# Attention and feed-forward kernel, Trainium2: the row of maxima by a DMA instead of a matmul and a VectorE copy, and the correction passes reordered around it

## What is computed

```python
Q = jnp.einsum('bnd,hdk->bhnk', x, proj_q)
K = jnp.einsum('bmd,dk->bmk', x, proj_k)
V = jnp.einsum('bmd,dv->bmv', x, proj_v)
logits = jnp.einsum('bhnk,bmk->bhnm', Q, K)
weights = jax.nn.softmax(logits, axis=-1)
O = jnp.einsum('bhnm,bmv->bhnv', weights, V)
Y = jnp.einsum('bhnv,hdv->bnd', O, proj_o)
# feed-forward, without a nonlinearity, 8 experts summed
mid = jnp.einsum('amh,ehn->aemn', x, w1)
out = jnp.einsum('aemn,enh->amh', mid, w2)
```

## Time and profile before

| | us |
|---|---|
| median of 3 runs | 1636.69 (1636.4 to 1636.76) |
| the profiled execution | 1637.05 |
| its span in the trace | 1635.2 |
| PE busy | 1618.8 (99%) |
| POOL busy | 1379.3 (84%) |
| ScalarE (ACT) busy | 1300.6 (80%) |
| VectorE (DVE) busy | 1229.2 (75%) |

### The profile page before, as it was taken

One profiled execution on the slowest core, in us unless ns is written; L12 is line 12 of the kernel. 1 busy time (PEld: TensorE's weight loads), 2 busy tenths in 40 slices (PEclk: granted clock), 3 DMA queues, 4 the chain that ended last, 5 costly groups with the idle time before them and its releaser, 6 DMA issues.

```text
span 1635.2 us, 46288 instructions
## 1 busy us (share of the span) xinstructions
PE 1618.8 (99%) x18686; PEld 1199.7 (73%) x18686; DVE 1229.2 (75%) x2605; ACT 1300.6 (80%) x1348; POOL 1379.3 (84%) x1008
## 2 busy tenths in 40 slices
PE   8999999999999999999999999999999999999998
PEld 6777777777777777777777777777777777777775
DVE  6777777777777777777777777777777777777775
ACT  4788888888888888888888888888888888878885
POOL 3688888888888888888888888888888888888786
PEclk9999999999999999999999999999999999999999
DMA  8000000000000000000000000000000000000000
GB/s 237 4 3 5 5 4 18 4 4 5 4 17 5 4 5 5 16 5 5 4 5 18 3 5 5 4 18 4 4 5 3 18 5 3 4 14 2 2 2 14
DMA packets 34690, 20.41 MB, mean 12 GB/s; under 512 B 18353, under 2 KB 30897, under 8 KB 34481
## 3 DMA queue, kind: packets, MB, share of 16 engines
q1 hardware_dynamic: 33440, 16.92, 3.9%
q10 hardware_dynamic: 1040, 0.52, 0.1%
HBM read 9.57 MB, written 4.19 MB: 8 GB/s over the span
## 4 chain that ended last, share of the span: by engine, by line
PE 97%; DVE 1%; ACT 1%; issue 0%; ACTq 0%; POOL 0%; DVEq 0%
PE s_ps L599 14%; PE s_ps L614 14%; PE s_ps L612 14%; PE t_ps L654 13%; PE t_ps L657 13%; PE t_ps L656 13%; PE s_ps L483 4%; PE s_ps L485 4%; PE s_ps L484 4%; PE t_ps L636 2%; PE t_ps L627 1%; PE t_ps L669 0%; PE s_ps L627 0%; DVE c_lo L970 0%; ACT pr_hi L446 0%; DVE xn L772 0%
## 5 line engine op out<-in xcount | busy, mean ns | idle before, releaser
L348 POOL TENSOR_TENSOR pr_lo<-pr,pr_hi 128x1024 f16<-128x1024 f32 x511 | 1079.6, 2135 | 228.3 <-ACT pr_hi L446 228.3
L439 ACT ACTIVATE pr<-s_ps,boost,scale 128x1024 f32<-128x1024 f32 x512 | 616.4, 1204 | 193.7 <-PE s_ps L614 193.6
L865 DVE TENSOR_REDUCE key_max<-s_ps 128x128 f16<-128x1024 f32 x512 | 624.0, 1219 | 0.2 <-PE s_ps L599 0.2
L446 ACT ACTIVATE pr_hi<-pr 128x1024 f16<-128x1024 f32 x512 | 525.5, 1051 | 8.2
L612 PE MATMUL s_ps<-g_lo,xT 128*128 128x128 f16 x4096 | 512.4, 219 | 1.0 <-DVE g_lo L878 1.0
L614 PE MATMUL s_ps<-g_hi,xT 128*128 128x128 f16 x4096 | 512.4, 219 | 0.0
L612 PEld LDWEIGHTS s_ps<-g_lo,xT 128*128 128x128 f16 x4096 | 400.4, 98 | 31.5 <-DVE g_lo L878 1.5
L614 PEld LDWEIGHTS s_ps<-g_hi,xT 128*128 128x128 f16 x4096 | 400.5, 98 | 29.9
L654 PE MATMUL t_ps<-pr_hi,xn_hi 128*128 128x512 f16 x1024 | 388.2, 379 | 1.8 <-DVE pr_lo L883 1.8
L657 PE MATMUL t_ps<-pr_hi,xn_lo 128*128 128x512 f16 x1024 | 388.2, 379 | 0.0
L656 PE MATMUL t_ps<-pr_lo,xn_hi 128*128 128x512 f16 x1024 | 388.2, 379 | 0.0
(11 more groups left out here) (126 smaller groups left out, 1545.3 us busy)
## 6 DMA issues: line engine op xcount, KB each, us to landing
out_dram<-xacc SPq DMA_DIRECT2D x16, 256.0 KB, 2.7
w_sb<-in_L_ffn_w_dram SPq DMA_DIRECT2D x1, 2048.0 KB, 9.5
xT<-xn_hi SPq DMA_TRANSPOSE x56, 2.2
xT<-xn_lo SPq DMA_TRANSPOSE x56, 2.4
pr<-in_L_attn_proj_q_dram ACTq DMA_DIRECT2D x1, 512.0 KB, 4.6
xacc<-in_L_attn_x_dram SPq DMA_DIRECT2D x2, 256.0 KB, 5.0
pr<-in_L_attn_proj_o_dram SPq DMA_DIRECT2D x1, 512.0 KB, 6.5
xacc<-in_L_attn_x_dram SPq DMA_DIRECT2D x1, 384.0 KB, 10.4
```

The lines of the kernel that those rows point to most:

```text
L348: pool.tensor_tensor(pr_lo[:, u % RING, :], pr32[:, u % PR, :], pr_hi[:, u % RING, :], ALU.subtract)\
L439: act.activation(pr32[:, u % PR, :], both_banks(u), ACT.Exp, bias=boost[:, 0:1], scale=scale[:, 0:1])\
L446: act.activation(pr_hi[:, u % RING, :], pr32[:, u % PR, :], ACT.Copy).then_inc(p_hi_ready, 1)
L865: dve.tensor_reduce(key_max[:, u % 2, :], both_banks(u).rearrange("p (t q) -> p q t", q=P), AX_X, ALU.max).then_inc(keys_max, 1)
```

## The change

The column of maxima is no longer turned by TensorE and copied by VectorE; SP waits for it and writes it as a row of 128 float16 numbers into row 0 of g_lo by a DMA from the 128 partitions. `low_passes` is cut into `low_keys` (keys' low by g_hi, needs no maximum) and `low_queries` (keys' high by g_lo, waits for the DMA). `low_keys` stands where the low passes began (in P1 it stands behind the projection, as before), `low_queries` stands late in the period, in P0, P1 and P3 behind the first product of place 1, in P2 behind all three. In P2 the first chunk of a block gives two products ahead of `turn_keys_max` instead of one. On VectorE `find_max` comes ahead of `between_maxima` in P1 and P2. SP runs one loop over the units: the bias DMA of each, a transpose at positions 1 and 2 of eight, the stores at positions 5 and 6 of every eighth pair.

```diff
-        minus_max = sb("minus_max", [P, 2, P], F16)
+        minus_max = sb("minus_max", [P, 2], F16)
...
+            def bias(u):
+                k, j = divmod(u, 4)
+                sp.wait_ge(max_found, u + 1)
+                if j == 0:
+                    sp.wait_ge(g_lo_ready, k + 1)
+                if u >= 1:
+                    sp.wait_ge(bias_in, 16 * u)
+                sp.dma_start(g_lo[0:1, k % 2, j * P:(j + 1) * P], minus_max[:, u % 2:u % 2 + 1]).then_inc(bias_in, 16)
...
+            for u in range(UNITS):
+                bias(u)
+                pair, at = divmod(u, 8)
+                if pair == 1 and at in (4, 5, 6, 7):
+                    turn(NT + at // 2 - 2, at % 2)
+                if at in (1, 2) and pair >= 2 and (tile := ln_tile(pair - 2)) is not None:
+                    turn(tile, at - 1)
+                batch = pair // H - 1
+                if pair % H == 2 and at in (5, 6) and batch >= 0:
+                    store(batch, at - 5)
...
-            def low_passes(u):
+            def low_keys(u):
                 k, j = divmod(u, 4)
-                pe.wait_ge(bias_ready, u + 1)
+                pe.wait_ge(keys_max, u + 1)
+                for t in range(NT):
+                    pe.matmul(bank(u, t // HT)[:, (t % HT) * P:(t % HT + 1) * P], x_lo(batch_tile(k) + t),
+                              g_hi[:, k % 2, j * P:(j + 1) * P], start=False, stop=False, skip_group_check=True)
+            def low_queries(u):
+                k, j = divmod(u, 4)
+                pe.wait_ge(bias_in, 16 * (u + 1))
                 if j == 0:
                     pe.wait_ge(g_lo_ready, k + 1)
                 for t in range(NT):
...
                 last.then_inc(scores_ready, 1)
...
             def turn_keys_max(u):
                 pe.wait_ge(keys_max, u + 1)
                 if u >= 1:
-                    pe.wait_ge(bias_ready, u)
+                    pe.wait_ge(max_found, u)
...
+                if u % 4 == 3 and summing(u - 1) >= 0:
+                    pe.wait_ge(t_lo_ready, summing(u - 1) + 1)
...
-            def max_to_row(u):
-                pe.wait_ge(max_found, u + 1)
...
                 if n < UNITS:
                     high_pass(n, 0)
-                if 1 <= n <= UNITS and at != 3:
-                    max_to_row(n - 1)
-                if n < UNITS:
                     high_pass(n, 1)
-                if 1 <= n <= UNITS and at == 3:
-                    max_to_row(n - 1)
                 if n == 0:
                     fold_c(1)
                 chunk(n, 0)
-                small_products(n)
+                if at == 1:
+                    small_products(n)
                 if 1 <= n <= UNITS:
-                    low_passes(n - 1)
+                    low_keys(n - 1)
+                if at != 1:
+                    small_products(n)
                 if at == 2:
-                    chunk(n, 1, rest=False)
+                    chunk(n, 1, (0, 1))
                 if n < UNITS:
                     turn_keys_max(n)
-                chunk(n, 1, first=at != 2)
+                chunk(n, 1, (2,) if at == 2 else (0,))
+                if 1 <= n <= UNITS:
+                    low_queries(n - 1)
+                if at != 2:
+                    chunk(n, 1, (1, 2))
...
             def find_max(u):
                 dve.wait_ge(turned, u + 1)
-                dve.tensor_reduce(minus_max[:, u % 2, 0:1], maxima_turned(u), AX_X, ALU.max, negate=True)\
+                if u >= 2:
+                    dve.wait_ge(bias_in, 16 * (u - 1))
+                dve.tensor_reduce(minus_max[:, u % 2:u % 2 + 1], maxima_turned(u), AX_X, ALU.max, negate=True)\
                    .then_inc(max_found, 1)
-            def place_bias(u):
...
             for n in range(PERIODS):
-                if 1 <= n <= UNITS:
-                    place_bias(n - 1)
                 if n < UNITS:
                     max_of_keys(n)
-                between_maxima(n)
+                if n % 4 in (0, 3):
+                    between_maxima(n)
                 if n < UNITS:
                     find_max(n)
+                if n % 4 in (1, 2):
+                    between_maxima(n)
```

More of the change, by code:

```diff
@@ L131, in attention_ffn @@
         g_ps, g_hi_ready, g_lo_ready = sem("g_ps"), sem("g_hi_ready"), sem("g_lo_ready")
-        high_done, keys_max, turned, max_found, rowed, bias_ready = (
-            sem(n) for n in ("high_done", "keys_max", "turned", "max_found", "rowed", "bias_ready"))
+        high_done, keys_max, turned, max_found, bias_in = (
+            sem(n) for n in ("high_done", "keys_max", "turned", "max_found", "bias_in"))
         scores_ready, exp_done, p_hi_ready, p_lo_ready = (
@@ L610, in low_passes @@
                 for t in range(NT):
[L611 to L615, removed]
+                    last = pe.matmul(bank(u, t // HT)[:, (t % HT) * P:(t % HT + 1) * P], x_hi(batch_tile(k) + t),
+                                     g_lo[:, k % 2, j * P:(j + 1) * P], start=False, stop=True, skip_group_check=True)
                 last.then_inc(scores_ready, 1)
@@ L626, in turn_keys_max, with weigh @@
                     pe.wait_ge(w1_evacuated, E)
+                if u % 4 == 3 and summing(u - 1) >= 0:
+                    pe.wait_ge(t_lo_ready, summing(u - 1) + 1)
                 pe.transpose(maxima_turned(u), key_max[:, u % 2, :], ident16[:, :]).then_inc(turned, 1)
-            def max_to_row(u):
-                pe.wait_ge(max_found, u + 1)
[L631 to L639, removed]
+            def weigh(k, t, products):
                 tile = (batch_tile(k) + t) % KEEP
@@ L644, in weigh @@
                 dst = sum_bank(k).rearrange("p (j c) -> p j c", j=4)
-                if first:
+                if 0 in products:
                     if t == 0:
@@ L650, in weigh @@
                             pe.wait_ge(t_lo_ready, k - 1)
-                        pe.wait_ge(bias_ready, min(4 * k + 6, UNITS))
+                        pe.wait_ge(max_found, min(4 * k + 6, UNITS))
                         if k == 1:
@@ L672, in fold_ffn, with chunk @@
                     last.then_inc(f_ps, 1)
-            def chunk(n, place, first=True, rest=True):
-                if n < 4 and rest:
+            def chunk(n, place, products=(0, 1, 2)):
+                if n < 4 and 2 in products:
                     turn_w1(2 * n + place)
-                if n in FOLDS and rest:
+                if n in FOLDS and 2 in products:
                     for e in range(2):
@@ L684, in chunk @@
                 if 0 <= k < BLOCKS:
-                    weigh(k, t, first, rest)
+                    weigh(k, t, products)
             def head_out(k, g):
```

26 lines of the change are left out of this document (9 added, 17 removed).

## The result

| | before | after |
|---|---|---|
| median, us | 1636.59 (4 runs) | 1773.34 (4 runs, 1771.54 to 1775.42) |
| ratio | | 1.0835, 95% interval 1.0822 to 1.0848 |
| span of the profiled execution, us | 1635.2 | 1771.3 |

Forecast were 1720 us, range 1700 to 1765: the direction was right, the size was not.

A forecast was written before the change was run, and what follows sets the result against it. PE, 99% busy, was taken as the bound, but after the change the loop behind W sets the pace: 54 blocks of 13.54 and 72 of 12.71 us give +82.1, with the end +83.2, so 1720 us; range 1700 to 1765.

The forecast's parts named there:

- the loop behind W: From W, a block's first weighing product in P2, through exponentials, p_high and POOL to the next: 13.54 or 12.71 us.
- the 1.15: In P2, late low_queries start the exponentials 1.35 instead of 0.20 us behind the first weighing product, lengthening the loop by 1.15.
- the hop back to PE: From the end of POOL's last p_low to PE's next first weighing product: between 0 and 0.14 us, taken as 0.05.
- The DMA: Bias copy from find_max's end to PE's start: bounded at 2.0 to 2.9 us, taken as 2.3, stalling PE 0.1 a block.
- The rooms: Time from find_max's end until low_queries is due, by unit: 2.3, 2.2, 2.5 and over 3.4 us.
- the rival that was worked out for 2.9: Bias DMA slow too, about 2.9 us: PE's blocks 13.2 and 13.35, short blocks +0.5, total 1755 us; chance 0.15.
- The start: Up to the first weighing product: 0.3 us of row matmuls saved, set against the first DMA landings; no net change.
- SP: SP's queue of bias DMAs, transposes and stores: a bias delayed by 0.5 us vanishes in PE's wait; nothing.
- The row matmuls and VectorE's copies: 512 row matmuls off PE save 28.7 us only if PE stays the bound; VectorE's copies, 142.8 us busy, no gain themselves.
- max_of_keys and the early turn: In P3 and P0 turn_keys_max comes at 1.89 us, its maximum ready at 1.90; 0.1 a block allowed.
- The end: From the last but one block's first weighing product to the last's: about 11.7 instead of 10.57 us, +1.1.
- What the profile would show: PE idle before the first weighing product, some 115 us, POOL's pr_lo as releaser; chain full of POOL's p_low.

The follow-up runs named there:

- the order alone: Kernel before, row matmul and VectorE copy kept, no bias DMA; only TensorE's order changed to that of the change: 1731.44 us, ratio 1.0576.
- the kernel with four pieces: Changed kernel with VectorE's 32 by 32 block transpose behind find_max, so the bias DMA moves four 64-byte runs: 1741.38 us, ratio 1.0637.
- the probes: Changed kernel with extra small DMAs of various shapes on the sync queue, to time their landings; kernel time not of interest, landings 1.55 to 2.8 us.
- the best kernel: Changed kernel with four 64-byte pieces, ScalarE's p_high ahead of the exponentials in P2, and the 3 MB x load in six parts: 1631.35 us, ratio 0.9967.

## Why the prediction was wrong in size, step by step

- **What bounds the kernel, and the loop behind W: right.** The chain was read correctly. The run with the order alone reproduces its length with the 1.15 added: 13.59 and 12.77 measured, 13.54 and 12.71 forecast. The term that was off is the hop back to PE, 0.10 where 0.05 was taken; over 126 blocks that is 6.3 us. The sum also took the first block as one of its kind; it is 3.0 longer (15.73 with the order alone; 14.54 before).
- **The DMA: the step that failed.** "I bound it at 2.0 to 2.9 ... and take 2.3, next to the transposes, whose payload is smallest." It took 2.86 from find_max's end to low_queries. The rooms were right (2.3, 2.2, 2.5, over 3.4; in the kernel with four pieces, where it hardly waits for the DMA, TensorE comes 2.38, 2.37, 2.45 and 3.41 behind find_max's end), and so was the rival that was worked out for 2.9, with its chance of 0.15: "PE's blocks become 13.2", measured 13.18, and "It decides from about 2.7 on". What failed was the choice inside the bounds by size in bytes. By the probes bytes don't decide at this size (one run of 256 B lands in 1.7, 512 B in pieces of four bytes in 1.9), while the shape does: a column of two-byte pieces written into a row takes 1.1 more than a column into a column. In 71 blocks without a normalisation this is 13.18 less 12.77, some 29 us; over all blocks, against the order alone, it is 1688.0 - 1656.2 = 31.8.
- **The fixed cost that the Trainium skill gives** for a DMA on GpSimd's path (DMA: Bandwidth & Descriptors, "Anatomy of one DMA — SWDGE (gpsimd) path", about 2.0 us) is near three of the four shapes here, 1.7 to 2.0 on SP's queue, and 0.8 below the one that the kernel uses. For that one the measurement decides.
- **The start: failed.** "The first landings have turn_w1 and the folds as cover, and I set the two against each other." The cover was there for a landing of 3 us. The queue was not looked at: the first bias DMA stood behind 3 MB of loads and landed after 12.2, and the clock fell to its lower level within the wait. The start got 11.1 us longer, where the prediction set it at nothing; the run with the load in six parts returns 10.3 of them. The range's upper end, 1765, had room for the slow DMA (1755 by its rival); without these 11.1 us the time would have been 1762.
- **SP: right otherwise.** A transpose or a store behind a bias does not lengthen its landing (median 2.78 with and 2.77 without). What did, by up to 0.7 in one unit of ten, goes with the instruction queues' packets, which the prediction doesn't mention.
- **The row matmuls and VectorE's copies: right as "no gain by itself".** The 28.7 us off PE were there and bought nothing as long as two longer loops stood.
- **max_of_keys and the early turn, "next to nothing; I allow 0.1 a block":** right for the changed kernel, where VectorE's copies are gone (11.4 us in front of the turn, 0.09 a block). In the kernels that kept them it was more: the run that puts the turn later in P3 returns 27.4 us, 0.21 a block.
- **The end: right**, 11.72 against about 11.7.
- **What the profile would show: partly wrong.** The chain does not run through POOL, since the waits of this kind are given as "issue", and PE waits mostly before low_queries: 120 us there by the distances between its starts, 19 in front of W, in 49 blocks, where some 115 were forecast. The waits for the DMA fall in the same blocks and use up most of what POOL's loop leaves. By the prediction's own test this meant that the DMA decides, which is true for the blocks without a normalisation.

The forecast's +83.2, plus 9.9 for the loop as the order alone shows it (1656.2 instead of 1646.3: the hop, the first block and some hundredths), 31.8 for the DMA and 11.1 for the start, give 136.0 of the 136.1. So two steps failed, the DMA's duration and the start set at nothing; the loop, the larger part, was right.

## What to carry to other kernels

A bound at 97 to 99% busy can have a second loop a tenth of a microsecond behind it: before an operation is moved, follow what it releases all the way round to the next wait of the bound engine, through every engine's written order, and write down the slack. For a small DMA in such a loop look at the shape, not the bytes: here 128 two-byte pieces into one partition were the slow one, and four runs gathered by VectorE the fastest. What the gathering engine does next comes later for it, so follow that as well. And look at what stands on its queue when it is issued for the first time.

## What the runs showed of the hardware that was not expected

- A copy of 128 two-byte pieces landed in 1.7 us from column to column, in 2.0 from row to column and in 2.8 from column to row, all 256 bytes on SP's queue. One run of 256 bytes took 1.7.
- From a column into one partition, 32 and 64 two-byte pieces took 1.90 and 2.14, but 128 four-byte pieces only 1.89 and four 64-byte pieces 1.55.
- All 51 of the later biases that landed after more than 2.95 us (3.5 at most) had packets of the instruction queues running beside them; of the 298 without such packets none took that long.
- A DMA issued behind a 3 MB load on the same queue landed after 12.2 us, though it moved 256 bytes.
- Within a wait of 9.41 us in the start, some 5 us into it, TensorE's granted clock fell to 0.50, and it stayed there for 10.2 us. The later waits in front of low_queries, several in each block and at most 1.1 us long, left it at 1.00.
- VectorE's 32 by 32 block transpose of 128x32 float16 took 0.21 us, and the copy of four 64-byte runs behind it was waited for 7 times in 512 in the best kernel.
